# Sorting the first part of a mixture of experts one attention step earlier: parts of 8 and 8 token tiles, row writes paced by column products, one register load per tile

## The reference, cut to what matters

```python
x = x + xattn0(layernorm(x), ctx)      # 8 heads
x = x + ffn0(layernorm(x))
x = x + xattn1(layernorm(x), ctx)      # 16 heads, then two dense layers
x = x + moe1(layernorm(x))             # 8 experts, the best 2 of each token
x = x + xattn2(layernorm(x), ctx)      # 8 heads
x = x + moe2(layernorm(x))
x = x + xattn3(layernorm(x), ctx)      # 1 head
x = x + moe3(layernorm(x))
```

## Time and profile before

| what | value |
|---|---|
| median of 3 runs | 875.87 us (874.03 to 876.32) |
| profiled execution: time, span | 878.39 us, 876.5 us |
| PE busy | 720.8 us, 82% of the span |
| DVE busy | 483.1 us, 55% |
| ACT busy | 394.7 us, 45% |
| POOL busy | 238.3 us, 27% |
| mean granted TensorE clock | 0.934 of full speed |

### The profile page before, as it was taken

How to read it: one execution, slowest core, us unless ns; L and a number is a source line. 1 busy time by engine, 2 the same in 40 slices (tenths; PEclk the granted TensorE clock), 3 DMA queues, 4 the chain that set the end, 5 groups by cost and what they waited for, 6 DMA issues and landing times. The chain is left out here.

```text
span 876.5 us, 14671 instructions
## 1 busy us (share of the span) xinstructions
PE 720.8 (82%) x4784; PEld 488.2 (56%) x4784; DVE 483.1 (55%) x1392; ACT 394.7 (45%) x837; POOL 238.3 (27%) x382
## 2 busy tenths in 40 slices
PE   1587888899988667978958787799999786779998
PEld 1355666566655435645525454567777675546665
DVE  4468676777777503623656874673335334444443
ACT  2465555466665525533424465353334554222221
POOL 4345454344321261224456643100001002000000
PEclk9999999999999977998967999799999999579999
DMA  9533224222230011222273320000000200023332
GB/s 294 140 96 86 64 65 117 70 69 68 76 85 16 11 46 46 88 82 82 70 193 87 90 75 2 1 1 1 1 0 1 82 0 1 1 79 104 97 94 63
DMA packets 76319, 57.94 MB, mean 66 GB/s; under 512 B 7400, under 2 KB 70120, under 8 KB 75768
## 3 DMA queue, kind: packets, MB, share of 16 engines
q1 hardware_dynamic: 74200, 52.85, 21.3%
q0 software_dynamic: 2048, 4.20, 1.5%
HBM read 25.37 MB, written 9.24 MB: 39 GB/s over the span
## 5 line engine op out<-in xcount | busy, mean ns | idle before, releaser
L909 DVE TENSOR_REDUCE negmax<-ps 128x2 f32<-128x512 f32 x256 | 169.8, 686 | 105.7 <-PE ps L1950 104.0
L1645 ACT ACTIVATE exps<-ps 128x512 f32<-128x512 f32 x256 | 148.3, 598 | 103.0 <-PE ps L1962 92.1
L1950 PE MATMUL ps<-stack 96*128 96x256 bf16 x512 | 102.6, 294 | 33.3 <-DVE negmax L909 19.3
L1962 PE MATMUL ps<-stack 99*128 99x256 bf16 x512 | 100.1, 286 | 22.6 <-DMA stack<-maxt 13.2
L1950 PEld LDWEIGHTS ps<-stack 96*128 96x128 bf16 x512 | 47.8, 103 | 58.2 <-DVE negmax L909 34.1
L1962 PEld LDWEIGHTS ps<-stack 99*128 99x128 bf16 x512 | 43.9, 101 | 63.8 <-DMA stack<-maxt 22.4
L1978 PE MATMUL ps<-exps,values 128*32 128x256 f32 x1024 | 72.9, 402 | 0.7 <-ACT exps L1645 0.7
L2203 PEld LDWEIGHTS ps<-pack_moe,ht 128*128 128x128 f32 x512 | 61.9, 191 | 15.8 <-issue 14.0
L1286 DVE SCALAR_TENSOR_TENSOR x_sb<-ps,weights,x_sb 128x128 f32<-128x128 f32 (+1 forms) x128 | 36.0, 344 | 61.7 <-PE ps L2203 61.6
L1819 ACT ACTIVATE ht<-ps,pack_moe 128x512 f32<-128x512 f32 x64 | 43.3, 686 | 57.5 <-PE ps L2291 56.0
L2203 PE MATMUL ps<-pack_moe,ht 128*128 128x128 f32 x512 | 62.3, 275 | 0.5 <-ACT ht L1819 0.5
(11 more groups left out here) (221 smaller groups left out, 1330.4 us busy)
## 6 DMA issues: line engine op xcount, KB each, us to landing
stack<-qk_parts SPq DMA_DIRECT2D x168, 128.0 KB
stack<-weights_t SPq DMA_DIRECT2D x32, 256.0 KB, 3.3
pack_moe<-in_moe SPq DMA_DIRECT2D x1, 3076.0 KB, 14.9
outputs_moe<-y_kept SPq DMA_DIRECT2D x46, 64.0 KB
ht<-gathered SPq DMA_DIRECT2D x22, 128.0 KB
gathered<-y_kept SPq DMA_DIRECT2D x10, 256.0 KB, 2.9
pack_moe<-in_moe SPq DMA_DIRECT2D x1, 2129.0 KB
pack_moe<-in_moe SPq DMA_DIRECT2D x1, 1732.0 KB, 6.9
```

The source lines that it names most:

```text
L909: dve.tensor_reduce(negmax_of[b % 2][:, :, h:h + 1].rearrange("p t h -> p (t h)"), ps[:, h % 2, :].rearrange("p (t k) -> p t k", t=2), AX, ...
L1645: nc.scalar.activation(exps[:, i, :], ps[:, 2 + h % 2, :], ACT.Exp, scale=scale)\
L1950: last = pe.matmul(ps[:, h % 2, t * T:(t + 1) * T], st[0:MAXROW, h, 0, t * P:(t + 1) * P], st[0:MAXROW, h, 1, :], start=True, stop=True)
L1962: last = pe.matmul(ps[:, 2 + h % 2, t * T:(t + 1) * T], st[0:MAXROW + 3, h, 1, t * P:(t + 1) * P], st[0:MAXROW + 3, h, 0, :], start=True, ...
```

## The change

FIRST_PART goes from 5 to 4, so that the first part has the 8 token tiles of batches 0 to 3 and the second part the other 8. The number of expert tiles stays 46, now 23 and 23. The first part is normalised, turned and ranked one step earlier: logits at (-1, 15) instead of (0, 12), the picks and places at (0, 1) to (0, 11) instead of (1, 1) to (1, 5); the weights follow at (1, 12). Tiles 8 to 13 are normalised in tail 2 and turned at (2, 13) and (2, 15); the last two before the first expert tile. The second part's picks and places come two tiles earlier (places at tile 7 instead of 9).

The first part's row writes are no longer two groups of ten at (1, 4) and (2, 4). They are issued one every second beat from (0, 14) on, and each waits for a column product two heads further on. The second part's are 16 instead of 12, and wait for tiles 5 to 20.

PE loads the column offsets of only three tiles at (2, 6), and then one offset after each tile's up product. `turn_max` gets two new waits, on `route_exp_in` for batch 6 and on `placed_ready` for batch 7, since logits and ranks now share its bank. ACT copies the turned tiles one beat later than PE turns them.

```diff
-FIRST_PART = 5
+FIRST_PART = 4
-NORMED = (range(0, 8), range(8, 10), range(10, NT))
-CHUNKS = ((0, 1, 2, 3), (4, 5, 6, 7), (8, 9), (10, 11, 12, 13), (14, 15))
+NORMED = (range(0, 8), range(8, 14), range(14, NT))
+CHUNKS = ((0, 1, 2, 3), (4, 5, 6, 7), (8, 9, 10, 11), (12, 13), (14, 15))
-SORT_STEPS = {"stats": ((-1, 6), (0, 3)), "rstd": ((-1, 7), (0, 4)), "norm": ((-1, 9), (0, 7)), "logits": (0, 12),
-              "top": (1, 1), "exp": (1, 1), "first": (1, 2), "second": (1, 3), "mark": (1, 3), "rank": (1, 7),
-              "place": (1, 4), "weigh": (1, 5), "load": (2, 6)}
-TURN_STEPS = ((-1, 11), (-1, 13), (0, 10))
-SEND_STEPS = ((1, 4, range(0, 5)), (2, 4, range(5, 10)))
+SORT_STEPS = {"stats": ((-1, 3), (2, 3)), "rstd": ((-1, 4), (2, 4)), "norm": ((-1, 8), (2, 6)), "logits": (-1, 15),
+              "top": (0, 1), "exp": (0, 2), "first": (0, 4), "second": (0, 6), "mark": (0, 8), "rank": (0, 9),
+              "place": (0, 11), "weigh": (1, 12), "load": (2, 6)}
+TURN_STEPS = ((-1, 10), (-1, 12), (2, 13), (2, 15))
+TURNED_STEPS = ((-1, 11), (-1, 13), (3, 0), (3, 1))
+SEND_FROM = 14
-SORT_BEATS = {"norm": (-1, 0), "turn": (0, 1), "logits": 2, "top": 3, "exp": 3, "first": (4, 5), "second": (6, 7),
-              "mark": 7, "rank": 7, "place": (8, 9, 11), "weigh": 10}
-EARLY_TILES = (34, 35, 37, 38, 40, 41, 43, 45)
-JOIN_TILES = (32, 33, 35, 36, 38, 40, 42, 43)
+SORT_BEATS = {"turn": -1, "logits": 0, "top": 1, "exp": 1, "first": (2, 3), "second": (4, 4), "mark": 5, "rank": 5,
+              "place": (6, 7, 9), "weigh": 8}
+EARLY_TILES = (33, 34, 36, 37, 39, 41, 43, 45)
+JOIN_TILES = (30, 31, 33, 34, 35, 37, 39, 40)
-SEND_TILE = 13
-FETCH_TILE = 27
+REGISTERS = 3
+SEND_TILE = 5
+FETCH_TILE = 25
...
                 if s in SORTED:
                     stats_all(s, len(NORMED) - 1, NORMED[-1])
+                    apply_all(s, len(NORMED) - 1, NORMED[-1])
                     sorted_tiles(s)
...
-                        for at_tail, at_beat, tiles in SEND_STEPS if nxt in SORTED else ():
-                            if (tail, u) == (at_tail, at_beat):
-                                send_rows(nxt, 0, tiles)
+                        n, odd = divmod(16 * tail + u - SEND_FROM, 2)
+                        if nxt in SORTED and not odd and 0 <= n < 2 * len(GROUPS[nxt][0]):
+                            send_row(nxt, 0, n // 2, n % 2)
...
+            def send_row(s, g, t, k):
+
+                n = 2 * (t - GROUPS[s][g][0]) + k
+                i, landed = sending(s, t, k)
+                if n == 0:
                     pool.wait_ge(zeros_out, 16 * ZEROINGS) if s == SORTED[0] and g == 0 else None
                     wait(pool, "placed_ready", s, 0, g)
...
+                if landed > 16:
+                    pool.wait_ge(sent[i], landed - 16)
+                if g:
+                    wait(pool, "taken_psum", s, 0, SEND_TILE + n)
+                else:
+                    done_heads = SEND_FROM + 2 * n - COL_BEAT[16]
+                    wait(pool, "cols_psum", "att" + s[3:], B - 2 + done_heads // 16, done_heads % 16)
+                at = bass.IndirectOffsetOnAxis(ap=placed[:, k, t:t + 1], axis=0)
+                pool.indirect_dma_start(gathered[g], at, z[:, t, :], None).then_inc(sent[i], 16)
...
             def turn_max(s, m):
                 wait(pe, "max_ready", s, m)
+                wait(pe, "placed_ready", "moe1", 0, 0) if (s, m) == ("att1", B - 1) else None
+                wait(pe, "route_exp_in", "moe1", 0, 0) if (s, m) == ("att1", B - 2) else None
...
                     if sort_at("load", tail, u):
-                        load_experts(nxt, 0)
+                        load_experts(nxt, slice(0, REGISTERS))
...
                     if 0 <= j + 1 < ALL_TILES:
-                        if j + 1 == PART_AT[1]:
-                            load_experts(s, 1)
                         pe.wait_ge(sem["taken_ready"], done("taken_ready", s, 0, j + 1))
...
                         pe.matmul(ps[:, (j + 1) % 2, :], taken_t[:, (j + 1) % 2, :], par(s, "experts")[:, bass.ds(at, 2 * T)],
                                   start=True, stop=True).then_inc(sem["up_psum"], 1)
+                        if j + 1 + REGISTERS < ALL_TILES:
+                            load_experts(s, slice(j + 1 + REGISTERS, j + 2 + REGISTERS))
```

More of the change, by code:

```diff
@@ L525, in turn_bank @@
             if s in SORTED:
-                return (TURN, TURN, TURN, 5, 6)[i]
+                return (TURN, TURN, 0, 1, 5)[i]
             return (0, 1, 0, 6)[i] if s in MOE else (6, SIDE, 6, 6)[i]
@@ L591, in ranks_at @@
             n = len(GROUPS[s][g])
-            return ps[:, (0, 5)[g], 0:(n + 1) * E].rearrange("p (n e) -> p n e", e=E)
+            bank, at = ((SIDE, P), (5, 0))[g]
+            return ps[:, bank, at:at + (n + 1) * E].rearrange("p (n e) -> p n e", e=E)
         def part_of(j):
@@ L1206, in beside_tile @@
                     route_pick(s, 1, (0,), at["first"].index(j))
-                if j in at["second"]:
-                    route_pick(s, 1, (1,), at["second"].index(j))
+                if j == at["second"][0]:
+                    route_pick(s, 1, (1,))
                 if j == at["mark"]:
@@ L1497, in attention @@
                         pool.tensor_tensor(kact, krelu, krelu, ALU.mult).then_inc(sem["kact_ready"], 1)
-            def send_rows(s, g, tiles):
-                if tiles[0] == GROUPS[s][g][0]:
+            def send_row(s, g, t, k):
+                n = 2 * (t - GROUPS[s][g][0]) + k
+                i, landed = sending(s, t, k)
+                if n == 0:
                     pool.wait_ge(zeros_out, 16 * ZEROINGS) if s == SORTED[0] and g == 0 else None
                     wait(pool, "placed_ready", s, 0, g)
[L1504 to L1512, removed]
+                if landed > 16:
[7 more added lines that the diff above has]
+                pool.indirect_dma_start(gathered[g], at, z[:, t, :], None).then_inc(sent[i], 16)
             def fetch_output(s, t, k):
@@ L1535, in sorted_tiles @@
                 make_rstd_all(s, len(NORMED) - 1, NORMED[-1])
-                send_rows(s, 1, GROUPS[s][1])
+                for t in GROUPS[s][1]:
+                    for k in range(2):
+                        send_row(s, 1, t, k)
                 for t in range(2 * FETCHED_EARLY):
@@ L1615, in beat @@
                 if nxt in SORTED:
-                    if (tail, u) in TURN_STEPS:
-                        copy_all(nxt, [TURN_STEPS.index((tail, u))])
+                    if (tail, u) in TURNED_STEPS:
+                        copy_all(nxt, [TURNED_STEPS.index((tail, u))])
                     if sort_at("exp", tail, u):
@@ L1874, in turn_all @@
                         wait(pe, "zt_ready", s, 0, 0)
-                    if s in SORTED and 0 < i < FIRST_CHUNK:
-                        wait(pe, "zt_ready", s, 0, i - 1)
+                    if s in SORTED and i == 1:
+                        wait(pe, "zt_ready", s, 0, 0)
                     for k, t in enumerate(chunks_of(s)[i]):
@@ L2039, in beat @@
                         wait(pe, "zt_ready", sn, n)
-                        wait(pe, "zt_ready", nxt, 0, FIRST_CHUNK - 2 + b - (B - 4)) if B - 4 <= b < B - 2 else None
+                        wait(pe, "zt_ready", nxt, 0, 1) if b == B - 4 else None
                         wait(pe, "ot_ready", st, b)
@@ L2092, in beat @@
                     if (tail, u) in TURN_STEPS:
-                        wait(pe, "qk_ready", FLOWS[flow][-1], 99)
-                        wait(pe, "hid_ready", FLOWS[flow][-1], B - 5 + (tail == 0))
+                        if tail < 0:
+                            wait(pe, "qk_ready", FLOWS[flow][-1], 99)
+                            wait(pe, "hid_ready", FLOWS[flow][-1], B - 5)
+                        else:
+                            wait(pe, "max_done", FLOWS[flow][-1], 99)
                         turn_all(nxt, [TURN_STEPS.index((tail, u))])
@@ L2099, in beat @@
                     if sort_at("rank", tail, u):
-                        wait(pe, "max_done", FLOWS[flow][-1], 99)
                         rank_tokens(nxt, 0)
                     if sort_at("load", tail, u):
-                        load_experts(nxt, 0)
+                        load_experts(nxt, slice(0, REGISTERS))
                 elif tail == 2 and u == 3:
@@ L2232, in _, with load_experts @@
             weights_at = {}
-            def load_experts(s, g):
-                tiles = slice(PART_AT[g], PART_AT[g] + TILES[g])
-                pe.wait_ge(sem["experts_ready"], done("experts_ready", s, 0, g))
+            def load_experts(s, tiles):
+                g = part_of(tiles.start)
+                if tiles.start == PART_AT[g]:
+                    pe.wait_ge(sem["experts_ready"], done("experts_ready", s, 0, g))
                 found = nc.values_load_multi_w_load_instructions(
@@ L2274, in sorted_tiles @@
                         last.then_inc(sem["y_psum"], 1)
-                    if j in SORT_BEATS["turn"]:
```

(3 more changed lines are left out.)

7 lines of the change are left out of this document (2 added, 5 removed).

## The result

The changed kernel takes 866.5 us (median of four runs, 861.4 to 869.8) where the kernel before took 876.1: a ratio of 0.9855, 95% interval 0.9815 to 0.9895. Forecast were 866.2. Run again beside the experiments it took 866.6, ratio 0.9861 (0.9802 to 0.9920). Its profiled execution took 869.78 us with a span of 868.0, against 878.39 and 876.5 before: 8.5 us of span to be found.

What follows compares the result with a forecast made beforehand. PE was taken to bound the expert tiles, a chain of small steps, partly at slow clock, att1's end. Terms -6.0 - 2.4 + 2.5 - 1.8 + 0 + 0 - 2.0 = -9.7 gave 866.2 us; range 858.5 to 882.

Steps and rivals of the forecast that it cites:

- Columns: Last batch's column products, first to eighth pair of heads: rid of late `finish` and dense row writes, -6.0 us (-8.5 to -1.8).
- The link between packed writes and late semaphores: End of att1: dense POOL row writes coincide with late PE semaphores at ACT and DVE; not shown, used with a discount.
- To the first tile: Last pair of columns to first expert tile: rows and PE's chain both ready at 12.7 us, -2.4 us (-3.1 to +1).
- Tail 0: Stage before the last columns: 27 sorting operations added on DVE, logits and transposes reduced, +2.5 us (0 to +5.4).
- DVE's lumps: Added sorting operations before batch 7's maxima come in lumps up to 2 us; beyond a 1.1 us beat they stall PE, +2.5.
- Tiles 0 to 11: First expert tiles: ranks' wait shrinks from 1.45 to 0.4 us, four token tiles fewer to normalise and turn, -1.8 (-3 to 0).
- Single loads: One register load after each expert tile's up product: 0.24 us each, hidden for 43 loads, 0; without cover +10 us.
- the cover of 0.4: Expert tiles: time a register load behind the up product may take without delaying the hidden transposes, put at 0.4 us.
- Where part 1 begins: Second part's first tiles: 8.3 us of load stop, row wait and slow clock traded for 8.2, net 0 (-3.4 to +1.5).
- A new wait of 4.8: Tile 23's transpose waits 4.8 us for the second part's sixteen row writes; 3.4 us of slow clock after it.
- hide in the 4.8: Rival, chance 0.05: dense writes bring 4 us late semaphores among expert tiles; before tile 23 its row wait absorbs them.
- Last tiles: Last expert tiles: part 0's outputs end four tiles earlier, so fetches start at tile 25 and catch up, -2.0 (-4 to 0).

## Why the prediction was right

- *Columns, -6.0, measured -6.4.* Right with its mechanism: the pacing pays about half, and the rest falls to the moved sorting, with PE's wait for `finish` gone. The link between packed writes and late semaphores, which I had discounted, holds for this stage. I misread one thing in the earlier trace rows: the wait of 3.99 us lies at the end of the ten writes, the last of which starts at 313.09, not in their middle.
- *To the first tile, -2.4, measured -2.2.* The rows are still what tile 0 waits for. The smaller load had no part in it: in bulk it cost nothing either.
- *Tail 0, +2.5, measured +0.8.* Mis-sized. DVE's lumps are there and PE waits 1.84 us once for a maximum, but the stage is hardly longer, and DVE is busy 82% of it and not above 90%. I priced each lump beyond a beat as lost, and the logits at 0.5 us gained, the shrinking alone; in fact their whole 2.30 us left the stage, and the step ahead, which has them now, grew by 0.15. How much each lump costs was not followed.
- *Tiles 0 to 11, -1.8, measured -1.9.* The number is right, its split is not: the ranks' wait fell from 1.45 to 0.97 us, not to 0.4, so the rest gave more than its 0.8.
- *Single loads, 0, measured 0.* 0.31 us each, above my 0.24 and under the cover of 0.4; tiles keep 1.64. What the floor of about 600 ns in the Trainium skill ("DMA: Bandwidth & Descriptors", latency and other measured facts) would have cost did not come: the rows have half of it. The loads' worth is larger than my line for them shows: -7.9 us in its stage when done alone, a gain that I had booked under the next line.
- *Where part 1 begins, 0, measured +2.9.* Above the bound of +1.5 (the second profile has +1.8), and the step is wrong. "A new wait of 4.8" at tile 23 was 1.1, at tile 24; instead the packed writes made semaphores late at tiles 13 to 17, and 9.8 were lost there. The failed sentence stands among the rivals: late semaphores before tile 23 "hide in the 4.8". They hid only in part: tiles that come later wait less for the rows, so the 4.8 shrank to 1.1, but what was lost ahead is twice the wait that could hide it, and POOL, waiting for semaphores too (2.15 us before the tenth write), sends the rows later. I had the mechanism, had seen it twice in att1, and did not ask what twelve to sixteen packed writes do among tiles where the kernel before had spaced them by one per tile.
- *Last tiles, -2.0, measured -4.0.* Under-sized, at its bound. The early fetches still lose 3.1 us to late semaphores between tiles 30 and 33.

So the total came out at 866.5 against 866.2 partly by luck. The stages that did better than forecast (last tiles by 2.0 us, tail 0 by 1.7, the columns by 0.4) cancelled part 1, which did worse by 2.9; the difference that is left in the profiled execution comes from the 2.4 us ahead of tail 0, nearly all in untouched code. By these tile 0 came 5.4 us earlier and not 8.

## What to carry to other kernels

A transfer that is moved or brought forward is not only late or early: ask how closely it now follows the one before. Among the tiles here, indirect writes packed at 1.26 us cost the other engines as much as the wait that they avoid (10 us either way), and more where there was no such wait (8 us in the kernel before); one per 1.64 us they cost nothing by themselves. So pace them by the consumer's own progress where there is time. When a queue is paced, look at every small operation that stands behind the new waits. Loads of registers of a busy engine were hidden here when made one at a time and three tiles ahead; other distances were not tried.

## What the runs showed of the hardware

- Beside indirect transfers that POOL issues 1.26 us apart, in the last columns and among the tiles, ACT, DVE and POOL waited for semaphores whose work was done: up to 4.0 us among the tiles (second profile of the changed kernel) and 4.8 in the columns (the kernel before with packed part-1 writes). In a row of six writes the first late semaphore fell due after the third; a row of three made one late by 0.9. Beside the last chain of att1 ten packed writes made none. In the stretches with one transfer per 1.64 us, six kernels with writes or fetches, no wait of this kind stands. Why is open: a busy POOL alone doesn't do it, transfers of another kind were not tried, nor a steady spacing between 1.26 and 1.64 us.
- A load of 23 registers took 2.35 us ahead of the tiles and 5.46 among them, 0.10 and 0.24 us a register. Three registers ahead of the tiles took 0.96, and one among them 0.30 to 0.41 (median 0.31; once 0.53, in the kernel before with single loads). Why the bulk load takes longer among the tiles is open.
- DVE's elementwise operations with two SBUF inputs took 0.59 to 1.08 us instead of 0.21 to 0.35 beside POOL's 128x512 products of 1.04 us; one with a single SBUF input (the write of expert_at) took 0.53 instead of 0.18. Reductions and operations that read PSUM kept their time.
